# Moving the third phase's weight and context transfers ahead of the routed expert stage

## The reference

```
x = x + L0_xattn(layernorm(x), ctx)   # 16 heads, distance bias
x = x + L0_ffn(layernorm(x))          # grouped routing, 8 experts + a shared one
x = x + L1_xattn(layernorm(x), ctx)   # attention over the heads of each row
x = x + L1_ffn(layernorm(x))          # top 2 of 8 experts, hidden 512
x = x + L2_xattn(layernorm(x), ctx)
x = x + L2_ffn(layernorm(x))          # int4-rounded weight + low-rank part
x = x + L3_xattn(layernorm(x), ctx)   # self-attention, cross-attention, two dense layers
x = x + L3_ffn(layernorm(x))          # top 2 of 8 experts, hidden 1024
```

## Time and profile before

| | |
|---|---|
| median of three runs | 1825.43 us |
| lowest, highest | 1821.39, 1826.34 us |
| profiled execution, its own time | 1828.24 us |
| span of the profiled execution | 1826.5 us |
| mean granted PE clock, as a share of full speed | 0.838 |
| bytes moved by DMA | 278.01 MB |

### The profile page before, as it was taken

One profiled execution on the slowest core, in us unless ns is written; L12 is line 12 of the kernel. 1 busy time (PEld: TensorE's weight loads), 2 busy tenths in 40 slices (PEclk: granted clock), 3 DMA queues, 4 the chain that ended last, 5 costly groups with the idle time before them and its releaser, 6 DMA issues.

```text
span 1826.5 us, 26133 instructions
## 1 busy us (share of the span) xinstructions
PE 1344.6 (74%) x8181; PEld 1085.0 (59%) x8181; DVE 809.6 (44%) x1978; ACT 431.3 (24%) x1096; POOL 257.9 (14%) x301
## 2 busy tenths in 40 slices
PE   5776686765553289999876675767459999999970
PEld 3444444534332288888654553555359999999970
DVE  2258788688687312212347365564621211112113
ACT  2545153252121011111231222223101111111110
POOL 2010020110100200000423424232210000000015
PEclk9887786786686699999897786879579999999995
DMA  9700010100650679888200101000068878888844
GB/s 346 252 1 1 1 57 0 43 15 23 204 190 0 215 269 302 290 276 293 89 8 12 46 9 48 0 15 9 0 248 320 319 306 311 320 320 315 306 185 124
DMA packets 101129, 278.01 MB, mean 152 GB/s; under 512 B 8640, under 2 KB 74336, under 8 KB 85856
## 3 DMA queue, kind: packets, MB, share of 16 engines
q1 hardware_dynamic: 94944, 260.73, 39.5%
q0 software_dynamic: 6144, 16.79, 2.8%
HBM read 222.96 MB, written 54.53 MB: 152 GB/s over the span
## 4 chain that ended last, share of the span: by engine, by line
PE 44%; issue 22%; DVE 13%; DMA 7%; POOL 6%; SPq 4%; ACT 3%; another core or an unknown queue 1%; DVEq 0%; POOLq 0%; ACTq 0%
PE bank L656 40%; DMA work<-in_moe 5%; POOL expert_rows_in L2148 2%; DVE stats L1382 1%; DVE work L1845 1%; DVE work L1376 1%; POOL rstd L2125 1%; POOL extra L2158 1%; PE bank L938 1%; DVE row_max L1438 1%; DVE extra L1595 1%; ACT norm_cols L1242 1%; DVE extra L1598 1%; POOL work L2158 1%; PE bank L897 1%
## 5 line engine op out<-in xcount | busy, mean ns | idle before, releaser
L656 PE MATMUL bank<-norm_cols,work 128*128 128x128 f32 x3744 | 466.3, 279 | 29.1 <-DMA work<-in_moe 27.5
L656 PEld LDWEIGHTS bank<-norm_cols,work 128*128 128x128 f32 x3744 | 453.5, 195 | 47.2 <-issue 30.9
L1376 DVE TENSOR_TENSOR extra<-bank,span 128x256 f32<-128x256 f32 x234 | 99.5, 425 | 526.3 <-ACT span L1215 526.3
L656 PE MATMUL bank<-work,extra 128*128 128x256 f32 x936 | 240.1, 380 | 0.0
L1215 ACT ACTIVATE span<-bank 128x256 f32<-128x256 f32 x234 | 89.9, 384 | 556.9 <-PE bank L656 556.9
L656 PEld LDWEIGHTS bank<-work,extra 128*128 128x128 f32 x936 | 160.7, 191 | 12.4
L656 PE MATMUL bank<-weights,norm_cols 128*128 128x512 f32 (+1 forms) x192 | 91.7, 629 | 8.5 <-ACT norm_cols L1242 5.7
L656 PE MATMUL bank<-work 128*128 128x256 f32 (+4 forms) x260 | 69.8, 419 | 26.2 <-ACT work L1242 10.4
L2118 POOL TENSOR_TENSOR rstd<-var_eps,neg_half 128x4 f32<-128x4 f32 x17 | 17.3, 1017 | 501.8 <-DVE var_eps L1388 501.8
L755 PE MATMUL bank<-ident,work 128*128 128x128 f32 x256 | 53.7, 369 | 36.1 <-DVE att_rows L1376 27.3
L1158 ACT ACTIVATE work<-bank,row_max 128x128 f32<-128x128 f32 x256 | 69.8, 392 | 42.2 <-DVE row_max L1438 42.1
(11 more groups left out here) (298 smaller groups left out, 1922.6 us busy)
## 6 DMA issues: line engine op xcount, KB each, us to landing
work<-in_moe SPq DMA_DIRECT2D x78, 1024.0 KB, 8.5
work<-in_moe SPq DMA_DIRECT2D x39, 2048.0 KB, 7.6
work<-in_moe SPq DMA_DIRECT2D x39, 512.0 KB, 6.1
expert_rows_in<-zero SPq DMA_DIRECT2D x3, 5504.0 KB, 36.0
expert_rows_out<-zero SPq DMA_DIRECT2D x3, 5504.0 KB, 33.6
att_cols<-expert_rows_in SPq DMA_DIRECT2D x78, 128.0 KB, 2.2
expert_rows_out<-att_rows SPq DMA_DIRECT2D x78, 128.0 KB, 6.3
ctx_rows<-in_ctx SPq DMA_DIRECT2D x8, 512.0 KB, 3.6
```

The lines of the kernel that those rows point to most:

```text
L656: return pe.matmul(o, l, r, start=a, stop=z)
L1376: return dve.tensor_tensor(o, a, b, op)
```

## The change

The 15 transfers leave `experts(1)`, where they followed the first tiles' loads. They now stand between `ctx_loads()` and the wait for the tile plan, behind a wait for the bank that `routed_end` fills. Everything else stays in its order.

```diff
                 load_rows(0, 2)
                 if layer == 1:
                     sp.sem_inc(sem("norm_rows_free"), 1)
-
-                    for dst, src in w3loads:
-                        sp.dma_start(dst, src).then_inc(sem("w3_loaded"), 16)
-                    sp.dma_start(CG[:, :, :], ctx_in[0:T, :, :].rearrange("t p n -> p t n")).then_inc(sem("ctx_loaded"), 16)
                 pair(start, 0, 0, False, True)
...
             ctx_loads()
+
+            b, n = job(jr1, ("dn",), 0)
+            sp.wait_ge(bank_full[b], n + 1)
+            for dst, src in w3loads:
+                sp.dma_start(dst, src).then_inc(sem("w3_loaded"), 16)
+            sp.dma_start(CG[:, :, :], ctx_in[0:T, :, :].rearrange("t p n -> p t n")).then_inc(sem("ctx_loaded"), 16)
             sp.wait_ge(sem("tiles_planned"), 1)
             sp.wait_ge(sem("results_zeroed"), 16 * yrows.shape[0])
             experts(1)
```

## The result

The changed kernel takes 1815.78 us (median of 4 runs, 1812.53 to 1816.19), the kernel before 1825.88 us in the same comparison (1821.39 to 1826.80). The ratio is 0.9946, with a 95% interval of 0.9926 to 0.9966: about 9.9 us less. The profiled execution took 1815.85 us, its span is 1814.1 us.

The account below looks back on a forecast made before the run. No engine bounds the whole; a PE, SP and DMA loop limits the stage, with a stall at tile 2. 9.1 + 1.4 = 10.5 us off 1825.43 gives 1814.9 us, range 1809 to 1820.5.

Parts of the forecast that it names:

- The sum: Whole kernel: 9.1 us at tile 2 plus 1.4 us in that pair, 10.5 us less, bounds 7.6 and 10.9.
- Where the transfers go, and what they run beside: Ahead of the tile plan: 15 issues in 8.0 us, 36 us of slack after them, first expert load not delayed.
- The price of 0 beside VectorE: Stretch 563 to 576: VectorE not slowed by the early transfers, 0 us taken; second bound 1.1 us.
- Tile 2: Tile 2's weight load: issued 4.7 us sooner, landing after 5.2 us; PE starts 9.1 us sooner, bounds 8.1 and 9.2.
- The estimate of 4.4 us: Landing time of tile 2's 1 MB load by the skill page's formula; would add 0.6 us of gain; not used.
- both costs: Ahead of tile 2: SP's time to issue the transfers and the DMA engines' time to carry them, both on the path.
- SP's part: Ahead of tile 2: 4.7 us of SP's issuing comes off the path, not the whole 8.0.
- The pair after it: Pair of tiles from tile 2's start: no half clock, 11.8 us in place of 13.2, gain 1.4, bounds 0.6 and 1.7.
- half a wait: In tile 2's pair: a wait of 0 to 0.7 us for the following pair's load; 11.8 us taken for the pair.
- the rival of slower pairs: Expert loop: it settles into pairs of 13.5 us, net 4.8 us slower, 1830.2 us; chance 0.06.
- The full stage: Rival, expert stage bounded by bytes: 4.19 MB less at 292 GB/s gains 14.3 us, 1811.1 us; chance 0.10.
- this rival: Tiles 2 to 5: a wait replaces the stall and drops the clock; gain 6.8 us with one, 3.1 with two; chance 0.13.

Follow-up runs that it names:

- e1: Changed kernel, with all 15 transfers also issued a second time in the old place: 1829.82 us against 1829.64 for the kernel before, ratio 1.0002.
- e2: Changed kernel, plus 15 tiny transfers of 8 KB each in the old place (SP's issuing without the bytes): ratio 0.9984 to the kernel before.
- e9: Kernel before, transfers in the old place, but 12 weights in one transfer with runs of 24 KB, 4 issues for 15: ratio 1.0009.
- e5: Against the kernel before: 14 weight transfers in the old stretch but on GpSimd's queue, the context transfer early on SP: ratio 0.9946.
- e4: Against the changed kernel: the 15 transfers moved behind tile 0's weight loads, ahead of the wait for the scattered rows; ratio 0.9987 to the kernel before.
- e8: Changed kernel, with SP reading expert numbers and row places ahead of its waits, for all expert loads and stores: 1810.04 us, ratio 0.9884 to the kernel before.
- e6: Changed kernel measured again without edit, the second comparison: 1819.96 us against 1832.07 for the kernel before, ratio 0.9937.
- e3: Kernel before, transfers in the old place, but 12 weights in one transfer with runs of 2 KB, 4 issues for 15: ratio 1.0016.

## Why the prediction was right, step by step

**The sum.** 10.5 us were forecast (bounds 7.6 and 10.9), 1814.9 us. Measured were 9.9 us by the first comparison and 11.5 by the second (0.0063 of 1832), 1815.78 us. The profile gives the change's two places 11.3 us, a little above the upper bound; the term that was too small is the pair after tile 2's start, below.

**Where the transfers go, and what they run beside.** Right. 15 issues in 7.9 us (8.0 forecast), the first expert load not delayed. The price of 0 beside VectorE was taken from a row with traffic of another kind; the changed kernel's row, 1.23 us beside 301 GB/s, the 48.34 against 48.33 us and e1's ratio bear it out.

**Tile 2.** The load was to go out 20.1 us after the first expert load, and went out at 19.89 and 19.21; 5.2 us of landing were forecast, 5.2 measured; tile 2 was to start at 25.5 us and started at 25.28. 9.1 us forecast, 9.3 measured. Taking the landing time from the load that had found the queue empty, and not the median, was right. The estimate of 4.4 us beside it rests on a fit that the Trainium skill, "DMA: Bandwidth & Descriptors", section "Anatomy of one DMA", gives for transfers issued by GpSimd. This load is issued by SP, and 5.2 us is what it took.

**How the stall was explained.** Here the argument was wrong in one step, though its sum was not. It said that both costs are on the path and took 4.7 us as SP's part. The two run side by side. SP's issuing alone delays tile 2 by 4.6 us (e2, 29.92 against 25.28); the bytes alone delay it by 8.8 us (e9, 34.11), nearly as much as both together, 9.3. Taking away SP's part alone, as far as e9 does so, brought 0.5 us and not 4.7, and even that is within what two profiles differ by (e1, which takes nothing away, has 33.88). Only because the change takes away both was the sum right.

**The pair after it.** 1.4 us forecast with a bound of 1.7; measured 1.93, outside. Two small terms: the four 128x256 matmuls after the half-clock ones were slow as well and had been left out of the sum, and the load for the following pair landed in time, where half a wait had been allowed for.

**The rest.** Waits of 17.4 us in the loop against 17.6: no sign of the rival of slower pairs. The full stage would have given 14.3 us; the first comparison's interval ends at 13.5 us and the second's at 15.6, and e2 speaks against it. No wait dropped the clock in this profile, where the longest in the loop was 1.80 us. That a stall of this kind does drop it was seen in e2 (5.16 us) and e5 (3.55 us; 2.93 us for the next 16 matmuls), and not at 0.67 us. In other profiles waits little longer than 1.80 us did drop it (last section), so this rival was closer than its one row in the kernel before made it look.

## What to carry to other kernels

Transfers that are wanted late belong where the DMA engines have nothing to do and no load that is wanted soon is queued behind them; an idle stretch shorter than their bytes only moves the stall (e4). A prefetch has two prices where it stands, the issuing engine's time and the bytes in its queue, and they overlap: fewer and larger transfers gained nothing while the bytes stood ahead of the load, and removing the bytes alone left half of the stall. In a loop in which PE frees a buffer, SP issues and DMA fills, it is worth trying to do ahead of SP's wait whatever can be done there: by the medians it gave 9.9 us here (e8 against e6), of which the profiles show 6.5 in the first expert stage and nothing in the second.

## What the runs showed of the hardware that had not been expected

SP's DMA issue is not of fixed length. Right behind a 3.1 MB transfer in runs of 2 KB, issues took 3.37, 2.13 and 2.17 us in place of 0.3 to 0.7 (e3); in runs of 24 KB the next four took 0.36 to 0.67, and the first held one was the 1 MB load, 4.69 us (e9). What exactly fills up, these runs don't show. Tiny transfers cost SP as much as large ones: 15 of 8 KB took 8.1 us, 15 of 256 and 512 KB 8.0.

A wait of PE near 2 us can go either way with the clock. Two waits of the same length, in e3 and in e8:

```profile
787.41 3.53 PE L656 MATMUL bank<-norm_cols,work 128*128 128x128 f32 x16 [1.89 <-DMA work<-in_moe]
```

```profile
732.13 2.05 PE L669 MATMUL bank<-norm_cols,work 128*128 128x128 f32 x16 [1.89 <-DMA work<-in_moe]
```

In the first expert stage of all these profiles every wait for weights of 1.92 us and more left the next 16 matmuls slow (2.87 to 3.78 us), and none of 1.88 us and less did. In the kernel before, the granted clock was 0.50 in 808 to 810, behind its wait of 2.09 us.
